# Moving the final residual add of each image from GpSimd to VectorE in a convolution and gated-FFN kernel

## What is computed

```python
x = x + conv_ref(ln_c(x), w, b, gamma, beta)    # 3x3 conv of sign(ln_c(x)) with binary weights,
                                                # batch norm over all images, relu
t = to_tokens(x)                                # 3136 tokens of 128 channels for each image
s = ln_t(t)
weights = einsum('bsd,do->bso', s, wr) + br     # router: one number for each token
_, idx = top_k(weights, k)                      # k = half of the tokens; k - 1 are used
h = gelu(einsum('bkd,dh->bkh', sel, w1) + b1)   # 128 -> 512 -> 128 on the chosen tokens
y = (einsum('bkh,hd->bkd', h, w2) + b2) * w_sel
t = t + (processed + s)                         # processed: y at the chosen tokens, else 0
```

## Time and profile before

| what | us |
|---|---|
| median of 3 runs | 2376.41 |
| lowest and highest of them | 2373.12, 2378.39 |
| the profiled execution | 2379.78 |
| its span on the core | 2377.8 |

### The profile page before, as it was taken

How to read it: one execution, slowest core, us unless ns; L and a number is a source line. 1 busy time by engine, 2 the same in 40 slices (tenths; PEclk the granted TensorE clock), 3 DMA queues, 4 the chain that set the end, 5 groups by cost and what they waited for, 6 DMA issues and landing times. The chain is left out here.

```text
span 2377.8 us, 38759 instructions
## 1 busy us (share of the span) xinstructions
PE 2202.0 (93%) x9739; PEld 1071.6 (45%) x9739; DVE 1622.5 (68%) x4887; ACT 1222.9 (51%) x2030; POOL 918.5 (39%) x714
## 2 busy tenths in 40 slices
PE   6999999966999999999999999998999999999997
PEld 3555555533444444444444444444444444444443
DVE  6777777755677766767676666666667676767764
ACT  4444444434555555555555555555555555555553
POOL 1000000024455544445445555454544454554433
PEclk9999999987999999999999999999999999999998
DMA  3444444431122222222222222222222222222201
GB/s 146 163 162 162 162 162 162 162 122 46 62 73 73 74 81 76 81 85 75 73 73 73 73 73 72 73 73 73 81 82 91 73 73 73 73 73 84 73 33 59
DMA packets 66710, 216.99 MB, mean 91 GB/s; under 512 B 28496, under 2 KB 33328, under 8 KB 62640
## 3 DMA queue, kind: packets, MB, share of 16 engines
q1 hardware_dynamic: 66464, 215.71, 25.1%
q10 hardware_dynamic: 144, 0.30, 0.0%
HBM read 136.70 MB, written 77.47 MB: 90 GB/s over the span
## 5 line engine op out<-in xcount | busy, mean ns | idle before, releaser
L950 PE MATMUL ps<-hs,w_c 128*128 128x448 f32 x1792 | 806.9, 564 | 0.8 <-ACT yo L505 0.6
L495 ACT ACTIVATE hs<-ps,b1c,undo 128x448 f32<-128x448 f32 x896 | 602.6, 718 | 136.6 <-PE ps L941 136.0
L412 POOL TENSOR_TENSOR tl<-tr,th 128x448 f16<-128x448 f32 x224 | 245.5, 1096 | 515.7 <-ACT th L518 393.9
L854 PE MATMUL ps<-yo,cwT 128*128 128x448 bf16 x2016 | 425.6, 356 | 0.0
L950 PEld LDWEIGHTS ps<-hs,w_c 128*128 128x128 f32 x1792 | 305.3, 192 | 191.7 <-issue 152.3
L505 ACT ACTIVATE yo<-ps,cols 128x448 f32<-128x448 f32 x224 | 141.9, 633 | 453.6 <-PE ps L950 453.6
L407 POOL TENSOR_TENSOR xb<-xb,zr 128x448 f32<-128x448 f32 x224 | 259.1, 1159 | 182.7 <-ACT zr L511 181.8
L419 POOL TENSOR_TENSOR yo<-yo,base 128x448 f32<-128x448 f32 x224 | 264.5, 1181 | 167.4 <-DVE yo L781 166.6
L939 PE MATMUL ps<-th,w_h 128*128 128x448 f16 x896 | 321.4, 359 | 0.0
L941 PE MATMUL ps<-th,w_l 128*128 128x448 f16 x896 | 319.3, 356 | 0.0
L940 PE MATMUL ps<-tl,w_h 128*128 128x448 f16 x896 | 319.2, 356 | 0.0
(11 more groups left out here) (131 smaller groups left out, 2709.7 us busy)
## 6 DMA issues: line engine op xcount, KB each, us to landing
xb<-x SPq DMA_DIRECT2D x31, 1568.0 KB, 7.6
xb<-x SPq DMA_DIRECT2D x33, 896.0 KB, 4.7
result<-yo SPq DMA_DIRECT2D x32, 896.0 KB, 4.4
y_int<-y SPq DMA_DIRECT2D x32, 784.0 KB, 3.7
xb<-x SPq DMA_DIRECT2D x33, 672.0 KB, 4.3
result<-yo SPq DMA_DIRECT2D x32, 672.0 KB, 3.4
y<-y_int SPq DMA_DIRECT2D x32, 448.0 KB, 5.3
y<-y_int SPq DMA_DIRECT2D x32, 336.0 KB, 4.8
```

Source lines behind the costliest of these rows:

```text
L412: nc.gpsimd.tensor_tensor(cut(tl, c), tr[(b + c) % 2][:, :], cut(th, c), ALU.subtract).then_inc(tl_ready, 1)
L495: nc.scalar.activation(hs[(b + slot) % 2][:, j, :], ps[:, H_BANK + j, 0:T], ACT.Gelu_apprx_tanh, bias=b1c[:, j:j + 1], scale=undo[:, 1:2]) ...
L854: last = M(bank, cwT[:, t, :], sg[b][:, c * ROWS + dy:c * ROWS + dy + ROWS, dx:dx + SIDE], start=t == 0, stop=t == TAPS - 1)
L950: last = M(bank, w2_c[:, j, :], hs[(b + c) % 2][:, j, :], start=first, stop=final)
```

## The change

`add_base` leaves GpSimd's program and enters VectorE's. Its operands, its two waits and its signal stay. It stands at the same positions, one behind each of `OUT_AT` (20, 25, 30, 34, 39, 46, 53), and there behind `next_candidate` and ahead of `take_router`, `token_base` and the next `count_above`. No DMA is moved and no buffer is added.

```diff
--- before.py
+++ after.py
@@ -412,13 +412,6 @@
-            def add_base(m, b, c):
-                g = m * NCH + c
-                pool.wait_ge(gated, g + 1)
-                pool.wait_ge(base_ready, g + 1)
-                nc.gpsimd.tensor_tensor(cut(yo[b], c), cut(yo[b], c), cut(base[b], c),
-                                        ALU.add).then_inc(out_ready, 1)
-
@@ -432,8 +425,6 @@
                         low_part(m, mb, c)
-                    for m, mb, c in due([p + 1 for p in OUT_AT], -1, n, b, pos):
-                        add_base(m, mb, c)
@@ -779,6 +770,12 @@
+
+            def add_base(m, b, c):
+                g = m * NCH + c
+                dve.wait_ge(gated, g + 1)
+                dve.wait_ge(base_ready, g + 1)
+                V.tensor_tensor(cut(yo[b], c), cut(yo[b], c), cut(base[b], c), ALU.add).then_inc(out_ready, 1)
@@ -807,6 +804,8 @@
                     for m, mb, r in rounds:
                         next_candidate(m, r)
+                    for m, mb, c in due([p + 1 for p in OUT_AT], -1, *at):
+                        add_base(m, mb, c)
```

## The result

| | changed | before |
|---|---|---|
| median of 4 runs, us | 2397.76 | 2376.00 |
| lowest and highest, us | 2392.70, 2399.88 | 2373.12, 2378.39 |
| profiled execution, us | 2399.88 | 2379.78 |
| its span, us | 2398.1 | 2377.8 |
| its mean granted clock | 0.980 | 0.981 |

The changed kernel is slower by the factor 1.0089 (95% interval 1.0070 to 1.0108), 21 us. The forecast was 2397.5. The page's row of busy time reads now

A forecast was written before the change was run, and what follows sets the result against it. TensorE's waits, not busy shares, were taken as the bound. Position 39's 12.7, back-edges' 4.9, clock's 3.2 and 0.7 for collisions and position 25, less 0.5 in the drain, made 21.0 us: median 2397.5, range 2388 to 2413.

The forecast's parts named there:

- What bounds the kernel: Whole kernel: only what makes TensorE wait moves the time; removing GpSimd's adds saves at most 0.5 us, in the drain.
- Position 39, 12.7 us: Between `next_candidate(1)` and `count_above(2)`, VectorE already late: the add costs 0.41 us in each of 31 images.
- The back-edges, 4.9 us: Add at position 53: VectorE reaches 12 loop back-edges 0.41 us later, lengthening TensorE's first wait there.
- The other five places, nothing: Positions 20, 25, 30, 34, 46: VectorE's idle time or slack covers the adds; at most 0.05 us at position 25.
- The slack ahead of round 4: Position 46: `count_above(4)` ends 1.36 us before TensorE asks, covering the add's 0.41 us.
- The clock, 3.2 us: Behind back-edges: longer first waits lower TensorE's granted clock more often, estimated as 3.2 us.
- the two more that the forecast puts behind back-edges: Two additional back-edges of the 12 show a lowered TensorE clock, at some 1.6 us each.
- The port: VectorE and GpSimd share an SBUF port; at position 39 VectorE's add starts first and GpSimd's L407 waits.
- The margin of 0.09 us: Position 39: VectorE's add would start at 1560.99, GpSimd's L407 at 1561.08.
- the 655 forecast: GpSimd's busy time was to fall to some 655 us in the changed profile.
- The first rival: Position 39: GpSimd gets the port first, 1.07 us more in about half the images, 17 us, 2414; chance 0.1.

The follow-up runs named there:

- experiment 4: Changed kernel with each of the seven adds at the end of its position, behind `count_above` instead of ahead: 2413.38 us, 1.0143 of the kernel before.
- experiment 5: Changed kernel plus a spare VectorE add of constants behind the add at position 39: 2451.24 us, 1.0305 of the kernel before.
- experiment 3: Kernel before with only the adds of chunks 0, 1, 2, 3 and 5 moved to VectorE: 2374.29 us, ratio 0.9989.
- 11: Kernel before with later requests (COUNT_AT, NORM_AT) and the adds of chunks 0, 1, 2, 3 and 5 on VectorE: 2368.47 us, ratio 0.9958.
- experiments 9 and 10: Four bodies per loop turn instead of two: in the kernel before 2385.55 us, ratio 1.0029; in the changed kernel 2402.65 us, ratio 1.0103.
- experiment 6: Changed kernel plus a spare GpSimd add of constants at the seven old places: 2436.06 us, 1.0242 of the kernel before.
- 7: Changed kernel with round 2 requested one position later (COUNT_AT[2] 43 instead of 42): 2391.66 us, 1.0062 of the kernel before.

## Why the prediction was right

**What bounds the kernel.** Right. The time was lost in the idle time of TensorE, at the two places named, and of the 239 us that GpSimd was relieved of only 4.4 came back, by a way that the prediction didn't see (below).

**Position 39, 12.7 us.** Right in mechanism and size: 0.41 us an image in the timeline, 12.6 us more idle time before round 2, 12.6 us by the kernel that moves this add alone. Undoing it at that place (experiment 4) brought round 2 back to 6.64 us, and a second add there (5) moved it on by what that add took, 0.54 us or 1.47.

**The back-edges, 4.9 us.** Right in kind, somewhat too large: the first wait rose from 1.10 to 1.43 us at the one shown (1.26 to 1.50 over all, 1.39 in the mean) where 1.5 had been said, the second stayed, and the waits grew by 4.0 us. Alone the add costs 3.3 us. The prediction took VectorE's pause as fixed, and it became 0.2 us shorter.

**The other five places, nothing.** Right in the sum for this table of requests (experiment 3), as a balance of small gains and losses, and not in general (11). At position 46 the add often meets GpSimd's L407: 17 of the 32 adds take over 0.7 us there, up to 1.37. The slack ahead of round 4, read as 1.36 us in the prediction, covers these too; its median is 0.5 us in the changed kernel.

**The clock, 3.2 us.** The number came near by luck. In the second phase the profile shows 9 low stretches of 49.0 us in all against 8 of 42.8 (the last and longest of each in the drain at the end), and TensorE's busy time rose by 3.9 us; at half the clock the 6.2 us more are 3.1 us, as an estimate. But the two more that the forecast puts behind back-edges aren't there: 3 of the 12 have a low stretch before the change and 3 after it, and the others come at waits for the rows or at `sum_counts`. The other three runs of the changed kernel had a mean clock of 0.981 to 0.985; the kernel before, run beside experiments 9 and 10, had 0.979 to 0.985. Experiment 4 shows the mechanism at full size: first waits of up to 2.35 us, a mean clock of 0.971, and 22.9 us more of busy time.

**What was not in the sum.** Two terms, of opposite sign. The cast ahead of the normalization rows waits for GpSimd less often: 4.4 us won. I had looked for such gains at `token_base` alone, since it is large, and passed over an operation of 0.26 us, which is the one that TensorE waits for. And the gate rows are waited for 4.5 us longer. From the request of these rows (L965) to the last step of their gate (L775) it takes 5.28 us in the mean instead of 5.18, as two small steps of the chain start 0.05 us later each. In the trace these two steps are late by 0.12 to 0.13 us in every second image of the loop and in no other, here and in experiments 4, 6 and 7, whose VectorE programs differ little from this one. In experiment 5, with one more VectorE instruction, they are never late, and the gate rows are still waited for 7.3 us. So they aren't the whole of it, and what delays them is open. That the sum came out within 1 us of the median is luck in part: these two terms cancel, and the clock's term stood where the busy time's growth is.

**The port.** At position 39 VectorE is first and L407 pays, as said, and its mean has risen from 1159 to 1237 ns. The margin of 0.09 us came as forecast: L407 starts 0.09 us behind the add in 18 of the 32 images and takes 1.52 us there. That is why GpSimd's busy time is 680 us and not the 655 forecast: 224 x 0.078 = 17 us of the 25. The first rival didn't come about, but experiments 4, 5 and 6 show it three times: a lead for GpSimd of 0.18, 0.23 and 0.37 us makes VectorE's operation of 0.26 to 0.62 us last 1.08, 1.39 and 1.55. The Trainium skill (SBUF — State Buffer, "Who interferes with whom") says that whoever issues first has the shared pair and the other fully blocks; these rows agree, and only leads below 0.09 us, as the one in the earlier trace rows, go against it. In the traces of all kernels here GpSimd was ahead of an add or a `token_base` of VectorE by 0 to 0.08 us 246 times, and VectorE got through in 212 of them; of the meetings with a lead of 0.09 to 0.5 us it got through in two.

## What to carry to other kernels

The busy share of an engine is not its room. Before work is moved to an engine that others wait for, look up at each place in its queue whether the next request on the bound engine finds it already late: there the operation costs its full time in the queue, and where there are 0.4 us of slack it costs next to nothing, until someone uses that slack. Look too at where the operation lands against the other engine's on the shared port, since 0.2 us decide between 0.6 and 1.4, and look at the small operations in a chain that the bound engine waits for: a cast of 0.26 us made 4.4 us of gain here and 21.7 us of loss in experiment 6. And where the bound engine waits for a chain of latencies, asking one step later (here 0.7% faster, by two tables) can be worth more than making an engine off that chain lighter.

## What the runs showed of the hardware

- An inserted f32 add of 128x448 takes 0.61 us in its row and 0.41 us of VectorE's queue when it stands between two small dependent operations.
- A cast of 28x224 elements takes 0.26 us alone and 1.08 us when GpSimd began an add of 448 columns 0.18 us before it.
- A hardware loop's back-edge isn't free and its price goes with the turn's length: VectorE pauses 3.0 to 3.7 us with two bodies and 6.7 to 7.8 us with four; TensorE not at all with two, and 5.0 us with four. The kernel with four was 6.9 us slower (2385.55 against 2378.65 us).
- The granted clock can fall to 0.5 (1.2 GHz) for some microseconds behind quite short waits of a busy TensorE. With first waits of 1.1 to 1.5 us it did so behind 3 of 12 back-edges, with 2.35 us behind all 12, and behind waits of 1.75 us for the normalization rows 17 times in experiment 6. With mean clocks of 0.971 and 0.968 instead of 0.980 TensorE is busy 22.9 and 24.0 us longer for the same 9739 matmuls. What else decides whether it falls isn't shown.
